# An LSTM over 1024 steps on one core: every product of its matrices in one scale, a scaled copy of h made by ScalarE, and plain two-column sums

## The reference

```python
# x: (2, 1024, 256), h0: (2, 256); 2 sequences, 1024 steps, D = H = 256
xW = einsum('ntd,dk->tnk', x, Wx) + b
for t in range(1024):
    a = xW[t] + h @ Wh                       # (2, 1024): i, f, o, g
    i, f, o = sigmoid(a[:, :256]), sigmoid(a[:, 256:512]), sigmoid(a[:, 512:768])
    g = tanh(a[:, 768:])
    c = f * c + i * g
    h = o * tanh(c)
x = x + hs
x = x + (shared experts + gated routed experts of x) / 4      # per token
```

## Time and profile before

| | us |
|---|---|
| three runs | 1886.73, 1886.88 (median), 1890.24 |
| span of the profiled execution | 1883.0 |
| first `h_hi` at, last `h_hi` at | 20.5, 1849.9 |
| one step (`h_hi` to `h_hi`) | 1.79 |
| busy: PE, PEld, DVE, ACT, POOL | 1807.7, 1604.6, 1543.3, 855.4, 121.4 |

### The profile page before, as it was taken

One profiled execution on the slowest core, in us unless ns is written; L12 is line 12 of the kernel. 1 busy time (PEld: TensorE's weight loads), 2 busy tenths in 40 slices (PEclk: granted clock), 3 DMA queues, 4 the chain that ended last, 5 costly groups with the idle time before them and its releaser, 6 DMA issues.

```text
span 1883.0 us, 111290 instructions
## 1 busy us (share of the span) xinstructions
PE 1807.7 (96%) x45674; PEld 1604.6 (85%) x45674; DVE 1543.3 (82%) x13293; ACT 855.4 (45%) x5545; POOL 121.4 (6%) x403
## 2 busy tenths in 40 slices
PE   9999999999999999999999999999999999999999
PEld 8888888888888888888888888888888888888888
DVE  7888888888888888888888888888888888888885
ACT  4564444444444444444444444444444444444442
POOL 0000000000000000000000000000000000000000
PEclk9999999999999999999999999999999999999999
DMA  6000000000000000000000000000000000000000
GB/s 250 4 4 4 4 7 4 7 4 4 7 4 7 4 4 7 4 7 3 7 4 4 7 4 6 4 4 7 4 7 4 4 7 4 7 4 6 4 4 8
DMA packets 7440, 20.85 MB, mean 11 GB/s; under 512 B 1168, under 2 KB 5648, under 8 KB 6160
## 3 DMA queue, kind: packets, MB, share of 16 engines
q1 hardware_dynamic: 6640, 13.60, 1.9%
q10 hardware_dynamic: 288, 0.13, 0.0%
HBM read 11.63 MB, written 2.10 MB: 7 GB/s over the span
## 4 chain that ended last, share of the span: by engine, by line
DVE 45%; PE 41%; ACT 9%; issue 5%; DVEq 0%
PE gates L835 16%; DVE gates L660 8%; DVE gates L644 8%; ACT gates L354 7%; PE gates L853 7%; DVE to L674 7%; PE gates L842 6%; DVE addend L656 6%; DVE hh L679 4%; DVE gates L675 3%; DVE gates L670 3%; PE acc_lg L879 2%; PE up_rt L873 2%; PE gates L861 2%; DVE hid_rt L629 2%
## 5 line engine op out<-in xcount | busy, mean ns | idle before, releaser
L853 PE MATMUL gates<-hh,wh_lo 128*128 128x24 f16 x8184 | 783.0, 183 | 0.0
L853 PE MATMUL gates<-hh,wh_hi 128*128 128x24 f16 x8184 | 783.0, 183 | 0.0
L853 PEld LDWEIGHTS gates<-hh,wh_hi 128*128 128x128 f16 x8184 | 549.4, 96 | 0.0
L853 PEld LDWEIGHTS gates<-hh,wh_lo 128*128 128x128 f16 x8184 | 548.3, 95 | 0.0
L354 ACT ACTIVATE gates<-gates 128x4 f32<-128x4 f32 x1024 | 161.8, 158 | 826.1 <-DVE gates L644 825.6
L835 PEld LDWEIGHTS gates<-hh,wh_lo 128*128 128x128 f16 x8184 | 271.6, 96 | 268.6 <-DVE hh L679 266.6
L861 PE MATMUL gates<-hh,wh_small 128*128 128x2 f16 x8184 | 489.1, 164 | 0.2 <-issue 0.2
L835 PE MATMUL gates<-hh,wh_lo 128*128 128x24 f16 x8184 | 380.3, 184 | 70.7 <-DVE hh L679 14.2
L644 DVE TENSOR_TENSOR_SCAN gates<-part_fac,gates 128x8 f32<-128x8 f32 x2048 | 295.3, 179 | 159.9 <-PE gates L842 138.8
L842 PE MATMUL gates<-hh,wh_hi 128*128 128x4 f16 x8184 | 370.0, 171 | 0.0
L861 PEld LDWEIGHTS gates<-hh,wh_small 128*128 128x128 f16 x8184 | 349.5, 96 | 0.3 <-issue 0.3
(11 more groups left out here) (230 smaller groups left out, 2594.4 us busy)
## 6 DMA issues: line engine op xcount, KB each, us to landing
rw_sb<-rw SPq DMA_DIRECT2D x2, 2048.0 KB, 22.1
sw_sb<-sw SPq DMA_DIRECT2D x3, 1024.0 KB, 13.6
x_sb<-xT SPq DMA_DIRECT2D x1, 1920.0 KB, 9.4
outT<-osb SPq DMA_DIRECT2D x15, 128.0 KB, 2.3
wh_sb<-wh SPq DMA_DIRECT2D x2, 512.0 KB, 4.4
wx_sb<-wx SPq DMA_DIRECT2D x1, 1024.0 KB, 6.0
x_sb<-xT SPq DMA_DIRECT2D x1, 128.0 KB, 5.0
eye_sb<-eye ACTq DMA_DIRECT2D x1, 64.0 KB, 4.2
```

Source lines behind the costliest of these rows:

```text
L853: mm(copies(q, m, LOW_COPIES)[:, :, :, 1], part, hh[:, c, half:half + 1, :].broadcast_to([P, LOW_COPIES, B]), start=False, stop=False, ski ...
```

## The change

- Before the loop, all of `wh_hi` and `wh_lo` are made gate by gate, all four with `wh_lo` times 4096 (before, O and I had `wh_lo` unscaled and a third matrix `wh_small`, which is gone). `unit`, the factor of the seeds, is 4096 times larger, so that all products and seeds stand in one scale.
- h has a third part, `h_up` = 4096 * `h_hi`, made by ACT in each step behind a wait for `h_hi`. PE's products with `wh_hi` take `h_up` and `h_lo` in place of `h_hi` and `h_lo`, and PE waits for it (`h_hi_scaled`).
- The two columns of F and of G now have the same scale, and `summed` is a plain sum over pairs (`tensor_reduce`, 8 elements to 4) in place of the scan.
- I and O keep one column each. The two matmuls that PE runs ahead of the wait for `h_lo` are of I, not of O, and stand behind a wait for the seeds of I. The order within a gate is: the `wh_lo` products, those with `h_up`, those with `h_lo`.
- DVE copies the seeds of I (4 elements) in the place where it made `c_now`, and those of O last in the step; before, O's were copied ahead of the wait for tanh c, and I's last. PE has a wait for each.
- `c_now` is made by ACT, right behind tanh c. tanh c is written into O's bank.

```diff
-        hh = sb("hh", [P, KC, 2, B], F16)
-        h_lo, h_hi = hh[:, :, 0, :], hh[:, :, 1, :]
+        hh = sb("hh", [P, KC, 3, B], F16)
+        h_lo, h_up, h_hi = (hh[:, :, j, :] for j in (LOW, UP, HIGH))
...
         @block.scalar
...
+            for q in WH_ORDER:
+                w = slice(q * D, (q + 1) * D)
+                activation(wh_hi[:, :, w], wh_sb[:, :, w], ACT.Identity, scale=wh_g if q == G else s_wh).then_inc(s_hi, 1)
+                activation(wh_times_lo[:, :, w], wh_sb[:, :, w], ACT.Identity, scale=unit if q == G else s_wh_lo).then_inc(s_hi, 1)
...
                 act.wait_ge(s_sum, 3 * s + C_OF)
                 activation(tc, cs[:, :, 2], ACT.Tanh, scale=0.5).then_inc(s_tanh, 1)
+                activation(c_now[:], cs[:, :, 2], ACT.Identity, scale=0.5).then_inc(s_tanh, 1)
+
+                if tile < NT - 1 or s < TS - 1:
+                    act.wait_ge(s_hhi, tile * TS + s + 2)
+                    activation(h_up, h_hi, ACT.Identity, scale=LO).then_inc(s_hup, 1)
...
         @block.vector
...
             def summed(dst, q):
 
-                return v.tensor_tensor_scan(dst, part_fac[:].rearrange("p c j -> p (c j)"), parts[q], 0.0, ALU.mult, ALU.add)
+                return v.tensor_reduce(dst, parts[q].rearrange("p (c j) -> p c j", j=PARTS), AX.X, ALU.add)
...
                 v.tensor_scalar(to1[:], to[:], 1.0, LO, ALU.add, ALU.mult).then_inc(s_own, 1)
-                v.tensor_copy(parts[O], seeds[:, piece % 2, at, O * HC:I * HC, :].rearrange("p c j -> p (c j)"))
-
-                dve.wait_ge(s_tanh, 3 * n + TC_OF)
+
+                dve.wait_ge(s_tanh, 4 * n + TC_OF)
...
                 if at == HS - 1:
                     dve.wait_ge(s_staged, tile * PIECES + piece + 2)
-                v.tensor_scalar(c_now[:], cs[:, :, 2], 0.5, None, ALU.mult)
+
+                dve.wait_ge(s_tanh, 4 * n + C_OFF)
+                v.tensor_copy(i_sum, seeds[:, piece % 2, at, I * HC:GATES, 1]).then_inc(s_seeded, 1)
 
                 dve.wait_ge(s_own, 2 * n + 2)
                 v.scalar_tensor_tensor(h_lo, h_hi, -LO, by_batch(h_now), ALU.mult, ALU.add).then_inc(s_hlo, 1)
 
-                v.tensor_copy(parts[I], seeds[:, piece % 2, at, I * HC:GATES, :].rearrange("p c j -> p (c j)")).then_inc(s_seeded, 1)
+                v.tensor_copy(o_sum, seeds[:, piece % 2, at, O * HC:I * HC, 1]).then_inc(s_oseeded, 1)
...
         @block.tensor
...
+            def in_one(q, w, half, n, at):
+
+                for m, c in at:
+                    dst = gates[:, q * BANK:q * BANK + n * APART].rearrange("p (r w) -> p r w", w=APART)[:, :, m * B:(m + 1) * B]
+                    last = mm(dst, block_of(w, q, m, c), hh[:, c, half:half + 1, :].broadcast_to([P, n, B]),
+                              start=False, stop=False, skip_group_check=True)
                 return last
...
                 pe.wait_ge(s_hhi, n + 1)
                 low(F)
                 low(G)
-                one_column(O, blocks[:EARLY // 2])
-
+                pe.wait_ge(s_seeded, n)
+                in_one(I, wh_lo, HIGH, LOW_COPIES, blocks[:EARLY])
+
+                pe.wait_ge(s_hup, n)
                 pe.wait_ge(s_hlo, n + 1)
                 high(F, 1).then_inc(s_mul, 1)
                 high(G, HIGH_COPIES).then_inc(s_mul, 1)
-                pe.wait_ge(s_seeded, n)
-                one_column(I, blocks)
-                and_low(I, 1).then_inc(s_mulio, 1)
-                one_column(O, blocks[EARLY // 2:])
-                and_low(O, 1).then_inc(s_mulio, 1)
+                in_one(I, wh_lo, HIGH, LOW_COPIES, blocks[EARLY:])
+                in_one(I, wh_hi, UP, LOW_COPIES, blocks)
+                in_one(I, wh_hi, LOW, 1, blocks).then_inc(s_mulio, 1)
+                pe.wait_ge(s_oseeded, n)
+                in_one(O, wh_lo, HIGH, LOW_COPIES, blocks)
+                in_one(O, wh_hi, UP, LOW_COPIES, blocks)
+                in_one(O, wh_hi, LOW, 1, blocks).then_inc(s_mulio, 1)
```

More of the change, by code:

```diff
@@ L167, in cond_resid_kernel @@
         tops, s_wh, s_wx, s_xin = scale[:, 0, :], scale[:, 3, 0:1], scale[:, 3, 1:2], scale[:, 3, 2:3]
-        sc = sb("sc", [P, 7])
-        unit, two_unit, to_tanh, half_lo, s_wh_lo, wh_g, wh_g_lo = (sc[:, j:j + 1] for j in range(7))
+        sc = sb("sc", [P, 6])
+        unit, two_unit, to_tanh, half_lo, wh_g, s_wh_lo = (sc[:, j:j + 1] for j in range(6))
         xw_scale = sb("xw_scale", [P, 2])
@@ L223, in cond_resid_kernel @@
         s_xwp0, s_xwc0 = sem("first_xw_product"), sem("first_xw_copied")
-        s_hhi, s_hlo = sem("h_hi_ready"), sem("h_lo_ready")
+        s_hhi, s_hup, s_hlo = sem("h_hi_ready"), sem("h_hi_scaled"), sem("h_lo_ready")
         s_mul, s_mulio, s_sum, s_tanh = sem("f_g_multiplied"), sem("i_o_multiplied"), sem("f_g_c_summed"), sem("f_o_c_tanh")
-        s_scan, s_seeded = sem("scan_operands_ready"), sem("i_seeds_in_place")
+        s_scan, s_seeded, s_oseeded = sem("scan_operands_ready"), sem("i_seeds_in_place"), sem("o_seeds_in_place")
         s_piece, s_staged, s_added = sem("piece_of_steps_done"), sem("piece_staged"), sem("h_added_to_x")
@@ L823, in _ @@
             mm = nc.tensor.matmul
+            blocks = [(m, c) for m in range(KC) for c in range(KC)]
             def copies(q, m, n):
@@ L838, in high @@
             def high(q, n):
-                for m in range(KC):
-                    for c in range(KC):
-                        last = mm(copies(q, m, n)[:, :, :, 0:2],
-                                  wh_hi[:, c, (q * KC + m) * P:(q * KC + m + 1) * P],
-                                  hh[:, c, :, :].rearrange("p (r j) b -> p r b j", r=1).broadcast_to([P, n, B, 2]),
-                                  start=False, stop=True, skip_group_check=True)
-                return last
-            def one_column(q, blocks):
-                for m, c in blocks:
-                    w = slice((q * KC + m) * P, (q * KC + m + 1) * P)
-                    for part, half in ((wh_lo[:, c, w], 1), (wh_hi[:, c, w], 1)):
-                        mm(copies(q, m, LOW_COPIES)[:, :, :, 1], part, hh[:, c, half:half + 1, :].broadcast_to([P, LOW_COPIES, B]),
-                           start=False, stop=False, skip_group_check=True)
@@ L856, in and_low @@
-            def and_low(q, n):
-                for m in range(KC):
-                    for c in range(KC):
-                        w = slice(((q - O) * KC + m) * P, ((q - O) * KC + m + 1) * P)
-                        last = mm(copies(q, m, n)[:, :, :, 1], wh_small[:, c, w], hh[:, c, 0:1, :].broadcast_to([P, n, B]),
-                                  start=False, stop=True, skip_group_check=True)
+                for m, c in blocks:
+                    last = mm(copies(q, m, n)[:, :, :, 0:2], block_of(wh_hi, q, m, c),
+                              hh[:, c, LOW:UP + 1, :].rearrange("p (r j) b -> p r b j", r=1).broadcast_to([P, n, B, 2]),
+                              start=False, stop=True, skip_group_check=True)
@@ L1007, in lstm @@
             def lstm(s, tile):
-                blocks = [(m, c) for m in range(KC) for c in range(KC)]
                 n = tile * TS + s
```

87 lines of the change are left out of this document (34 added, 53 removed).

## The result

The changed kernel takes 2003.57 us, median of four runs (1998.15 to 2010.32), beside 1886.81 us (1886.66 to 1890.24) for the kernel before: a ratio of 1.062, interval 1.060 to 1.063. The forecast was 1945 us, 1927 to 1967: slower as foreseen, but by 117 us instead of 58, and outside the range.

What follows compares the result with a forecast made beforehand. The bound was taken as one round through all engines, 97% of the span. Wait +77 less reduction 20 gave 57 ns a round over 1023 rounds, +58 us: span 1941.3 plus 3.9, 1945 us, range 1927 to 1967.

Steps and rivals of the forecast that it cites:

- (c): PE's separate wait ahead of `high`, in all 1023 rounds: costs 77 ns a round, bounds 60 and 90.
- Rivals A: Separate wait on PE hidden behind the ten early matmuls, only (a) left: -20.5 us, 1866 us; chance 0.06.
- C: Separate wait on PE costs its 51 ns less some 35 of overlap: +15 a round, 1902 us; chance 0.04.
- (a): DVE's sums of f and g by reduction: 159 ns, a gain of 20 ns a round, bounds 11 and 28.
- Rival B: DVE's reduction is no faster than the scan: 77 a round, +78.8 us, 1966 us; chance 0.07.
- (b): PE's early products of I: I's last product 50 ns sooner; alone gains nothing, lets (a) through.
- (d): ACT's `h_up`: 201 ns, ends at 0.40, before `h_lo` releases PE at 0.48; cost zero.
- (e): ACT's `c_now` behind tanh c: ends 0.06 after `h_hi` starts, needed at 0.14; cost zero.
- Rival D: ACT's `h_up` comes last: needs 0.33 us against 0.20, each 10 ns beyond costs 10 us; chance 0.02.
- (f): DVE's seed copies of I (0.14 to 0.30) and O (from 0.34) are in time; cost zero.
- (g): Conversions on ACT and DVE before the loop: between -0.3 and +0.5 us, taken as 0.
- Rival E: PE's clock falls through 0.09 us more idle time a round: 1 us a round, more than 2000 us; chance 0.01.

Runs made afterwards that it cites:

- the mended kernel: Changed kernel with one count for `h_up` and `h_lo`, `hh` padded to four parts, I and O written to every second column: 1882.46 us, ratio 0.9987.

## Why the prediction was half right

**(c), the separate wait: right.** 77 ns were taken; the median `high` starts at 0.570 in the changed kernel instead of 0.480, and the same wait alone costs 74 ns a round in the kernel before. Step 64's 0.09 gave it, and its partial return came too: the second matmul of `high` follows the first by 0.025 us instead of 0.037. It is 76 of the 117 us. Rivals A (hidden) and C (35 ns) fall with it: it is hidden only where what it waits for is there early.

**(a), the reduction: the term was mis-sized.** 20 ns were taken, 5 are there: the reduction takes 174 ns, not 159, which is above the upper bound of 168 too. L584 (8 to 1, SBUF, 151) was a poor row for an operation with four results in PSUM, and its line with L480 had no point with several results. Rival B, which gave 0, was nearer: 5 ns off, where the forecast was 15 off. The section Rules for kernel authors of "VectorE: DVE Perf Modes" in the Trainium skill, which calls a reduction the slowest DVE operation, is not borne out to the letter, as the reduction is 4 ns shorter than the scan; by it the gain would have been nothing, which is nearer to what was measured than the forecast was. 15 ns a round, 15 us, were missed here.

**(b), the early pair: its own term right.** 0 was said for it alone, and no difference over 0.5 us was measured with the pair of O put back. It was said to let (a) through, and isn't needed for that: with O's pair the round is 1.784 us, and L646 and tanh i both end at 1.335 (medians), 0.035 before the scan for c.

**(d) and (e): right.** `h_up` takes 207 ns (201 taken) and ends at 0.40; `c_now` is over 0.05 after `h_hi` starts. Rival D didn't occur. **(f)** held: the copies of the seeds, at 0.14 and 0.34, are in time. **(g)** too: the first `h_hi` stands at 20.54 against 20.53.

**Not in the sum at all: the layout of `hh`.** The diff shows it, a 2 that becomes a 3, and the part by part account has no term for it. It costs 12 ns a round alone and up to 17 in the other pairs of runs; alone in the kernel before it is 14 us.

**Not as an addition: the clock.** Rival E had it fall because PE waits longer in a round, for the whole run, at a chance of 0.01. The rival's reason was wrong, as the separate wait alone keeps 1.00, and so was its form: the clock falls for some rounds at most tile starts and costs some 29 us on top of what else is changed. Its price was wrong as well: rounds of the changed kernel that lie wholly at half the clock take 1.92 to 2.45 us, 0.05 to 0.6 more than its median, not 1 us more. The largest step that failed is that the sum has the clock at nothing, on the argument that PE "waits in every round of these 100 us (released at 0.21 and 0.48) and keeps 1.00": that argument answers the wait, and rightly, but those 100 us show 24 columns written to every second, and the change altered those columns. No window of the kernel before would have priced it, as it keeps 1.00 between two tiles too (361 to 363 above); it took a run with the columns changed.

By this the sum is 74 (wait) + 14 (layout of `hh`) - 5 (reduction) = 83 ns a round, against 85 in the trace; times 1022 that is 85 us, and with the 29 us of slow rounds and 1 of the tail 115 of the 117. Without the clock the changed kernel would stand near 1975 us, so the two misses in the round, 15 and 14 us, were enough to leave the range, which ended at 1967.

| part of the change | taken | shown | by |
|---|---|---|---|
| separate wait for `h_lo` | +79 us | +76 us | alone in the kernel before |
| sums by a reduction | -20 us | -5 us | scan in the mended kernel |
| three parts in `hh` | not seen | +14 us | alone in the kernel before |
| I and O side by side | not seen | +29 us | slow rounds in the trace after; alone +31 (median; +19 to +34 by run) |
| early pair, `c_now`, `h_up`, seeds | 0 | 0 | early pair undone; timeline |
